# Causal attention on Trainium2: leaving out the masked columns of the diagonal score tiles

## The reference, cut to what matters

```python
latent = einsum('btc,rc->btr', x, basis_w)                # rank 64, shared by all heads
lt  = einsum('btr,hrs->bhts', latent, head_mats)          # the head's query
att = einsum('bhts,bus->bhtu', lt, latent) / sqrt(64)     # the keys are the latent itself
att = softmax(where(tril, att, -inf))                     # causal: u <= t
y   = (att @ v) @ o_w.T + o_b
x   = layernorm(x + y)
h   = gelu(x @ (alpha1 * sign(w1)).T + b1)
x   = layernorm(x + h @ (alpha2 * sign(w2)).T + b2)
```

## Time and profile before

| | |
|---|---|
| time before, median of the runs shown | 3793.95 us (2 runs, 3776.59 and 3811.31) |
| profiled execution, its own time | 3739.45 us |
| its span, first to last instruction, slowest core | 3737.7 us |
| spans of the 8 cores | 3694.5 to 3737.7 us |
| mean granted TensorE clock of the cores | 0.77 to 0.79 of 2.4 GHz |

### The profile page before, as it was taken

The page is one execution under the profiler, slowest core; times in us unless marked ns, Lnnn a source line. Parts: engine busy times, 40 slices in busy tenths (PEclk is TensorE's granted clock), DMA queues, the critical chain, the costliest instruction groups (busy, mean ns, idle before and its releaser), DMA issues.

```text
span 3737.7 us, 36843 instructions; the slowest of 8 cores (3694.5 to 3737.7 us)
## 1 busy us (share of the span) xinstructions
PE 2293.7 (61%) x12698; PEld 1207.0 (32%) x12698; DVE 1320.4 (35%) x2058; ACT 1196.2 (32%) x1455; POOL 92.5 (2%) x158
## 2 busy tenths in 40 slices
PE   1212475857667477675756567665767667676665
PEld 0000142424243242422434343433324343332443
DVE  2556515342324403244153424243242423334200
ACT  0233133512545035450223123331335225462210
POOL 1011000000000000000000000000000000000000
PEclk9555688878788787887878787887879788887877
DMA  6899132222231131212323222321322221212233
GB/s 132 244 251 258 41 94 76 84 74 58 70 93 55 53 91 43 88 44 64 85 64 98 82 58 74 96 73 53 84 62 82 65 63 57 79 57 62 76 110 107
DMA packets 331548, 327.25 MB, mean 88 GB/s; under 512 B 16621, under 2 KB 304365, under 8 KB 331370
## 3 DMA queue, kind: packets, MB, share of 16 engines
q1 hardware_dynamic: 302362, 303.80, 27.0%
q0 software_dynamic: 29008, 21.11, 3.9%
HBM read 310.96 MB, written 25.17 MB: 90 GB/s over the span
## 4 chain that ended last, share of the span: by engine, by line
PE 43%; DMA 21%; DVE 16%; ACT 12%; issue 7%; POOL 1%; DVEq 0%; SPq 0%; ACTq 0%; POOLq 0%
PE pF L963 11%; PE pSX L908 10%; DMA sw2b<-sw2scr 8%; ACT Pp L685 7%; DMA sw1b<-sw1scr 5%; PE pO L701 4%; PE pSW L791 4%; PE pO L583 3%; PE pSW L651 3%; DMA sw2scr<-x2T 3%; PE pO L705 3%; DMA sw1scr<-x2T 3%; DVE bnsc L763 2%; PE pSX L651 2%; DVE lrec L711 2%
## 5 line engine op out<-in xcount | busy, mean ns | idle before, releaser
L963 PE MATMUL pF<-hbuf,sw2b 128*128 128x256 bf16 x4096 | 637.8, 310 | 205.4 <-DMA sw2b<-sw2scr 198.7
L908 PE MATMUL pSX<-x2T,sw1b 128*128 128x256 bf16 x4096 | 512.1, 283 | 151.4 <-DMA sw1b<-sw1scr 127.6
L963 PEld LDWEIGHTS pF<-hbuf,sw2b 128*128 128x128 fp8e4 x4096 | 432.9, 110 | 428.3 <-issue 306.6
L908 PEld LDWEIGHTS pSX<-x2T,sw1b 128*128 128x128 fp8e4 x4096 | 386.7, 101 | 276.9 <-issue 208.8
L685 ACT ACTIVATE Pp<-pSW,negmc 128x1024 bf16<-128x1024 f32 x320 | 357.0, 1115 | 249.8 <-DVE pSW L666 99.1
L662 DVE SCALAR_TENSOR_TENSOR pSW<-pSW,masks 128x512 f32<-128x512 f32 x128 | 89.5, 699 | 894.6 <-PE pSW L655 894.6
L685 ACT ACTIVATE Pp<-pSX,negmc 128x1024 bf16<-128x1024 f32 x320 | 356.5, 1114 | 110.8 <-PE pO L705 64.5
L924 ACT ACTIVATE hbuf<-pSX,b1c_s,al1c 128x256 bf16<-128x256 f32 x512 | 288.7, 567 | 249.7 <-PE pSX L908 249.4
L701 PE MATMUL pO<-Pp,Vt 128*65 128x512 bf16 x640 | 296.1, 463 | 106.4 <-ACT Pp L685 106.1
L651 PE MATMUL pSW<-qp,latd 64*128 64x512 bf16 x320 | 146.5, 458 | 315.3 <-ACT Pp L685 167.9
L705 PE MATMUL pO<-Pp,Vt 128*65 128x512 bf16 x640 | 285.2, 446 | 0.0
(11 more groups left out here) (104 smaller groups left out, 2081.8 us busy)
## 6 DMA issues: line engine op xcount, KB each, us to landing
sw2b<-sw2scr SPq DMA_DIRECT2D x512, 256.0 KB, 2.7
sw1b<-sw1scr SPq DMA_DIRECT2D x128, 512.0 KB, 4.1
xres<-hs SPq DMA_DIRECT2D x32, 512.0 KB, 4.5
out<-outb SPq DMA_DIRECT2D x32, 512.0 KB, 2.7
xT<-hsT POOLq DMA_DIRECT2D x16, 512.0 KB, 6.9
hbuf<-w1n SPq DMA_DIRECT2D x16, 512.0 KB, 8.5
hbuf<-w1t SPq DMA_DIRECT2D x16, 512.0 KB, 9.7
y2t<-w1t SPq DMA_DIRECT2D x16, 512.0 KB, 10.8
```

The costliest lines, as they stand in the source:

```text
L908: bank=bank, toff=toff: e.matmul(bank[:, 0:HF], sw1b[par][:, k, 128 * cl:128 * cl + 128], x2T[:, k, toff:toff + HF], start=(k == 0), stop= ...
L963: stp=stp: e.matmul(bank[:, boff:boff + HF], sw2b[par][:, hcl, 128 * dc:128 * dc + 128], hbuf[:, hc, :], start=stt, stop=stp),
```

## The change

In a diagonal tile D0 to D3 the first 0, 128, 256 or 384 query columns lie wholly before every key of the tile: all their scores are masked. The change gives each tile an offset `off` (0, 128, 256, 384; 0 for all other tiles) and leaves the first `off` columns out of the score matmuls, of the two masks, of the exponential and of the two matmuls with the values.

For an offset over 0 the columns to be kept are no longer one run of 1024. The exponential is then two instructions, one for each head.

```diff
+        def joff(j):
+            return 128 * (j - TT * ci) if j >= TT * ci else 0
...
             P.op("tensor", lambda e, j=j, bA=bA, off=off: e.matmul(
-                bA[0:128, 0:TC], latd[0:64, 128 * j:128 * j + 128],
-                qp[0:64, :], start=True, stop=True, tile_position=(0, 0)),
+                bA[0:128, off:TC], latd[0:64, 128 * j:128 * j + 128],
+                qp[0:64, off:TC], start=True, stop=True,
+                tile_position=(0, 0)),
...
-                    bA[:, 0:TC], bA[:, 0:TC], 1.0, masks[:, o, :],
+                         bA[:, off:TC], bA[:, off:TC], 1.0,
+                         masks[:, o, off:TC],
...
-            if TC == 512:
+            if TC == 512 and off == 0:
                 P.op("scalar", lambda e, dst=dst, par=par: e.activation(
                     dst[:, 0:2 * TC], SBKW[par][:, 0:1024], AF.Exp,
                     bias=negmc[:, 0:1]), waits=ew, inc="act")
             else:
-                    dst[:, 0:TC], bA[:, 0:TC], AF.Exp, bias=negmc[:, 0:1]),
-                    waits=ew, inc="act")
+                    dst[:, off:TC], bA[:, off:TC], AF.Exp,
+                    bias=negmc[:, 0:1]), waits=ew, inc="act")
-                    dst[:, TC:2 * TC], bB[:, 0:TC], AF.Exp,
+                    dst[:, TC + off:2 * TC], bB[:, off:TC], AF.Exp,
                     bias=negmc[:, 0:1]), inc="act")
...
-                pO[0:65, 0:TC], vv[:, j, h0, :], Pp[par][:, 0:TC],
-                start=(j == 0), stop=(j == JT - 1)), waits=[("act", ed)],
+                     pO[0:65, off:TC], vv[:, j, h0, :], Pp[par][:, off:TC],
+                     start=(j == 0), stop=(j == JT - 1)),
+                 waits=[("act", ed)], inc="pe")
...
-                pO[0:65, 512:512 + TC], vv[:, j, h1, :], Pp[par][:, TC:2 * TC],
+                     pO[0:65, 512 + off:512 + TC], vv[:, j, h1, :],
+                     Pp[par][:, TC + off:2 * TC],
```

More of the change, by code:

```diff
@@ L650, in emit_S @@
             gB = "pS2" if par == 0 else "pS4"
-            P.op("tensor", lambda e, j=j, bA=bA: e.matmul(
-                bA[0:128, 0:TC], latd[0:64, 128 * j:128 * j + 128],
-                qp[0:64, :], start=True, stop=True, tile_position=(0, 0)),
+            off = joff(j)
+            P.op("tensor", lambda e, j=j, bA=bA, off=off: e.matmul(
+                bA[0:128, off:TC], latd[0:64, 128 * j:128 * j + 128],
+                qp[0:64, off:TC], start=True, stop=True,
+                tile_position=(0, 0)),
                 waits=[("act", q_evac[0])] + guard(gA, gB), inc="pe")
-            P.op("tensor", lambda e, j=j, bB=bB: e.matmul(
-                bB[0:128, 0:TC], latd[64:128, 128 * j:128 * j + 128],
-                qp[64:128, :], start=True, stop=True, tile_position=(64, 0)),
+            P.op("tensor", lambda e, j=j, bB=bB, off=off: e.matmul(
+                bB[0:128, off:TC], latd[64:128, 128 * j:128 * j + 128],
+                qp[64:128, off:TC], start=True, stop=True,
+                tile_position=(64, 0)),
                 inc="pe")
@@ L661, in emit_S @@
                 o = j - TT * ci
-                P.op("vector", lambda e, o=o, bA=bA: e.scalar_tensor_tensor(
-                    bA[:, 0:TC], bA[:, 0:TC], 1.0, masks[:, o, :],
[L664 to L668, removed]
+                P.op("vector", lambda e, o=o, bA=bA, off=off:
+                     e.scalar_tensor_tensor(
+                         bA[:, off:TC], bA[:, off:TC], 1.0,
+                         masks[:, o, off:TC],
+                         op0=ALU.mult, op1=ALU.add), waits=[("pe", sm)],
+                     inc="dve")
+                P.op("vector", lambda e, o=o, bB=bB, off=off:
+                     e.scalar_tensor_tensor(
+                         bB[:, off:TC], bB[:, off:TC], 1.0,
+                         masks[:, o, off:TC],
+                         op0=ALU.mult, op1=ALU.add), inc="dve")
                 s_done[j % 2] = ("dve", P.c("dve"))
@@ L700, in gen_attn_pair @@
             vv = Vt[:].rearrange("p (g h v) -> p g h v", g=c.GT, h=H)
-            P.op("tensor", lambda e, j=j, par=par, vv=vv, h0=h0, JT=JT: e.matmul(
-                pO[0:65, 0:TC], vv[:, j, h0, :], Pp[par][:, 0:TC],
-                start=(j == 0), stop=(j == JT - 1)), waits=[("act", ed)],
-                inc="pe")
-            P.op("tensor", lambda e, j=j, par=par, vv=vv, h1=h1, JT=JT: e.matmul(
-                pO[0:65, 512:512 + TC], vv[:, j, h1, :], Pp[par][:, TC:2 * TC],
-                start=(j == 0), stop=(j == JT - 1)), inc="pe")
+            P.op("tensor", lambda e, j=j, par=par, vv=vv, h0=h0, JT=JT,
+                 off=off: e.matmul(
+                     pO[0:65, off:TC], vv[:, j, h0, :], Pp[par][:, off:TC],
+                     start=(j == 0), stop=(j == JT - 1)),
+                 waits=[("act", ed)], inc="pe")
+            P.op("tensor", lambda e, j=j, par=par, vv=vv, h1=h1, JT=JT,
+                 off=off: e.matmul(
+                     pO[0:65, 512 + off:512 + TC], vv[:, j, h1, :],
+                     Pp[par][:, TC + off:2 * TC],
+                     start=(j == 0), stop=(j == JT - 1)), inc="pe")
             st_["pp_free"][par] = P.c("pe")
```

5 lines of the change are left out of this document (3 added, 2 removed).

## The result

| | before | after |
|---|---|---|
| device time, median | 3740.12 us (10 runs, 3719.89 to 3811.31) | 3637.25 us (11 runs, 3622.36 to 3696.26) |
| span of the profiled execution | 3737.7 us | 3644.9 us |

The ratio is 0.9731, with a 95% interval of 0.9705 to 0.9756. The medians differ by 102.9 us; the forecast was 97. The two runs that were shown before (3811.31 and 3776.59) turned out to be the two highest of ten, and I had set the forecast from their median. Some executions are slow, with a lower granted clock on the cores of one half of the chip (two of the changed kernel, 3689.97 and 3696.26 us, with 0.74 to 0.75 on cores 0 to 3), and the two runs shown, 1.5% and 2.5% above the fastest of the ten, look like such executions, though their clocks are not on record.

The account below looks back on a forecast made before the run. No engine fills the span; the diagonal tiles wait on the latency of matmul, masks and exponential. Gains of 48 x 1.9 = 91, plus 6, plus 0, make 97 us off 3793.95: 3697 us, range 3640 to 3770.

Parts of the forecast that it names:

- The level: Whole kernel: the 97 us gain was taken from the shown runs' median, 3793.95, giving 3697 us.
- rival C: All 48 later pairs gain 2.4 us, the first chunks 16 and 8: 139 us, so 3655; chance 0.05.
- Late chunks: Chunks two to four of both sequences: 48 pairs at 1.9 us each, 91 us gained.
- D0 to copy: Time from D0's exponential to the pair's closing copy: about 4.5 us forecast where the pair read had 6.44.
- The chain: Diagonal tiles wait on matmul, two masks, exponential, twice over; shortening each link ends the pair read 1.97 us earlier.
- the fill: Between D1's and D2's value matmuls: starts about 3181.25, takes 1.04 us, just fits with nothing to spare.
- Durations: Diagonal tiles, 384, 256 and 128 columns: exponentials 0.58, 0.47, 0.36 us; masks 0.555, 0.42, 0.28 us.
- Second sequence's first chunk: Eight pairs where a fill's weight load hides most of the gain: 0.75 us each, 6 us.
- Very first chunk: First sequence's first chunk, eight pairs: DMA transfers hide the change, so nothing gained.
- Rival A: Later chunks: fills and their loads become the pace, each pair gains 0.97 us, 47 in all, so 3747; chance 0.24.
- Rival B: The 48 pairs: TensorE's granted clock falls, 10 us a pair per whole unit; 0.28 lower gives 3831; chance 0.05.
- the last value matmuls: D3's two value matmuls, at the pair's end, lose 384 columns each: 0.32 us a pair.

Follow-up runs that it names:

- v1: Against the kernel before, only the value matmuls leave the masked columns out; 1.0035 of the time before, 1.0033 in the repeat.
- v4: The change with the score matmuls whole again; 0.9777 of the time of the kernel before.
- x4: The change with a third buffer for the feed-forward weights sw2b; 0.9239 of the time of the kernel before.
- v2: Against the kernel before, value matmuls and masks leave the columns out, scores and exponentials whole; 0.9895 of the time before.
- v3: Against the kernel before, value matmuls and exponentials leave the columns out, scores and masks whole; 0.9931 of the time before.
- w: The change with score and value matmuls whole, so only masks and exponentials are shortened; 0.9742 of the time of the kernel before.

## Why the prediction was right and wrong

**The level, wrong.** The step that failed is "The median of the runs shown is 54.5 us above it, 3793.95; I forecast 3697 against that", and with it the range. The runs shown were two; ten have a median of 3740.12, within 1 us of the profiled execution's 3739.45. The low end of the range, 3640, was set 15 us under rival C, whose 3655 counts from the same 3793.95, and so was too high by the same step. Had I set the sum against the profiled execution, as the same paragraph does first (3642 for its like), the time would have been 5 us off.

**The gain, right.** 97 us forecast, 102.9 between the medians; 2.6% and 2.7%. The traces of the two profiled executions show less, 93 us in the span of the slowest core and 89 in the mean of the cores.

**Late chunks, right in size.** 48 x 1.9 = 91 forecast, 92 measured. D0 to copy fell by 1.91 us in the mean of the 48 pairs (1.97 worked out for the pair read, which was one of the short ones: 6.44 us, where the mean was 7.46). The chain was the right model: v1 to v4 move it by 0.41, 0.96, 1.26 and 1.79 us, where it said 0.32, 0.84, 1.06 and about 1.87. One reading in it is a little off: the fill does not "end as D2's exponential does" but, by the same figures, at 3181.25 + 1.04 = 3182.29, 0.2 us behind it; in the trace it is 0.3 us, and the value matmuls of D3 did not wait for it.

**Durations, right.** Exponentials 0.58, 0.47 and 0.37 us against 0.58, 0.47 and 0.36; masks 0.56, 0.43 and 0.29 against 0.555, 0.42 and 0.28. By the rule of the Trainium skill ("ScalarE: Activation LUTs", section "What ACT_TABLE_LOAD costs"), about 280 ns plus 0.833 ns a column with a bias pointer, the exponentials would take 0.60, 0.49 and 0.39, an estimate. The trace after is 0.02 below it each time.

**Second sequence's first chunk, half right.** 6 us forecast, 2.7 measured. That the wait for the weights covers the gain there was right, as x4 shows; the 0.75 us a pair that I left uncovered was too much (0.34 measured). I counted TensorE's columns ahead of the first fill at 1.2 GHz and left out that the fill itself could slow: in the changed kernel the sixth pair's fill took 1.92 us, and the one in the earlier trace rows 1.60. That accounts for 0.3 us in the one pair read; whether it does so in all eight was not read.

**Very first chunk, right.** Nothing forecast; it moved by +2 us, and the kernel before, profiled twice, differs by 4 there.

**Rival A, refuted** in the late chunks by x4. **Rival B, right as a mechanism, wrong on this change.** I took 10 us for a unit of clock from one pair of rows; the same reading over all late pairs of the kernel before gives 11, and v1 against it 12.6 with what follows the fourth pairs counted in. The clock fell by only 0.005 here, and masks and exponentials became shorter together with the matmuls: with the matmuls alone it is 0.783 (v1), with masks or exponentials added 0.807 (v2, v3), with both 0.822 (v4). Where the matmuls alone were cut, what rival B says came true in its direction: v1 is slower than before, by 0.3%.

**What the sum had by luck.** I counted 0.32 us a pair for the last value matmuls. It is on the chain, but w, which leaves these matmuls and the scores whole, takes the same time at a higher clock. The sum has no term for the clock. The forecast of the late chunks needed the clock to stay, and it did (0.825 and 0.820); the prediction's reason for that, that TensorE's busy share hardly moves, was not tried by any run.

## What to carry to other kernels

In a stretch where no engine is full, work out the chain through one tile and ask of each cut what it takes off that chain; busy time saved says little. Cutting matmul columns by themselves may bring nothing or cost a little, as v1 did here, when the granted clock falls with them; cut the links that TensorE waits for, and compare the granted clock of the same stretch before and after. Set a forecast against the profiled execution when few other runs are known.

## What was not expected of the hardware

With over a third of the diagonal tiles' value columns gone (768 of 2048) and nothing else changed, TensorE's granted clock in the late stretches went from 0.825 to 0.783 and, on another chip, from 0.830 to 0.772, and the kernel became 0.3% slower. With all columns kept and shorter waits it went to 0.858. The fall was deepest between two pairs, from the closing copy to the next query copy (0.85 to 0.70). One unit of that clock is worth 11 to 13 us in a pair of 20 to 30 us. What in TensorE's stream the clock answers to was not separated here: the columns, the gaps between them, and where the gaps fall all changed at once.

A ScalarE instruction over two separate runs of PSUM columns costs about what the line through instructions over one run gives for the same total: 0.686 us for two runs of 256 columns, against 0.85 ns x 512 + 0.25 = 0.69 us, an estimate from the earlier trace rows. No run here has an exponential over one run of 512 columns.
